# Emptying and clearing the PSUM banks of a graph kernel's counts two at a time

## The reference

```python
h = jnp.maximum(_layernorm(x), 0.0)
agg_src  = segment_sum(h[src], dst, 6250)          # round 0, features of the sources
agg_edge = segment_sum(edge_attr_128, dst, 6250)   # features of the edges
x = x + relu(concat([h, agg_src, agg_edge]) @ L0_W.T + L0_b)
h = jnp.maximum(_layernorm(x), 0.0)
for W_l, b, W_r in ((W1_l, b1, W1_r), (W2_l, b2, W2_r)):   # rounds 1 and 2
    agg = segment_sum(h[src], dst, 6250) / maximum(degree, 1)
    h = relu(agg @ W_l + b + h @ W_r)
x = x + h
```

## Time and profile before

| | us |
|---|---|
| median of 3 executions | 2033.34 |
| lowest, highest | 2031.09, 2033.35 |
| span of the profiled execution, first to last instruction | 1450.0 |
| the rest of the median, before and after the span | 583.3 |
| build, start of the first and of the last step (L997) | 120.8, 662.7 |
| TensorE matmul busy in the span | 1368.8 |
| ScalarE busy in the span | 490.1 |

### The profile page before, as it was taken

One profiled execution on the slowest core, in us unless ns is written; L12 is line 12 of the kernel. 1 busy time (PEld: TensorE's weight loads), 2 busy tenths in 40 slices (PEclk: granted clock), 3 DMA queues, 4 the chain that ended last, 5 costly groups with the idle time before them and its releaser, 6 DMA issues.

```text
span 1450.0 us, 34753 instructions
## 1 busy us (share of the span) xinstructions
PE 1368.8 (94%) x12165; PEld 1235.0 (85%) x12166; DVE 812.4 (56%) x1837; ACT 490.1 (34%) x1389; POOL 654.9 (45%) x772
## 2 busy tenths in 40 slices
PE   3777999999999999998999999999999999999996
PEld 3656999999999899997888888888888888888885
DVE  8686898888888888882454545432222222221221
ACT  2632123455688888882333232311111110000000
POOL 5400000011121121215777777167777745777775
PEclk9988999999999999999999999999999999999998
DMA  6108778888999988886565556566666665666663
GB/s 182 29 2 221 202 221 230 242 248 237 261 271 266 273 260 260 262 269 222 161 214 177 175 199 162 193 195 196 205 196 207 187 194 190 220 210 214 213 203 74
DMA packets 284762, 295.12 MB, mean 204 GB/s; under 512 B 19461, under 2 KB 250064, under 8 KB 284672
## 3 DMA queue, kind: packets, MB, share of 16 engines
q1 hardware_dynamic: 233861, 212.90, 46.9%
q0 software_dynamic: 26016, 69.24, 16.9%
q10 hardware_dynamic: 24795, 11.74, 2.8%
HBM read 245.70 MB, written 48.11 MB: 203 GB/s over the span
## 4 chain that ended last, share of the span: by engine, by line
PE 84%; POOL 2%; issue 2%; DMA 2%; ACT 2%; DVE 0%; ACTq 0%; POOLq 0%; DVEq 0%; SPq 0%
PE edge_banks L1065 41%; PE edge_banks L1023 20%; PE banks L997 10%; PE edge_banks L1096 4%; PE edge_banks L1019 4%; PE banks L1083 3%; POOL shared L833 2%; ACT shared L1252 1%; DMA shared<-in_edge_attr 1%; PE edge_banks L1072 1%; PE banks L1077 1%; ACT banks L1247 0%; DMA shared<-g_rows,list_src 0%; DMA shared<-counts 0%; ACT shared L1229 0%
## 5 line engine op out<-in xcount | busy, mean ns | idle before, releaser
L833 POOL DMA_INDIRECT shared<-g_rows,list_src x555 | 541.9, 976 | 230.8 <-issue 167.2
L1065 PE MATMUL edge_banks<-g_even,shared 128*128 128x257 f16 (+1 forms) x3822 | 444.7, 273 | 4.4 <-DMA shared<-counts 4.4
L1065 PEld LDWEIGHTS edge_banks<-g_even,shared 128*128 128x128 fp8e3 x3822 | 372.4, 97 | 62.6 <-issue 4.6
L1023 PE MATMUL edge_banks<-shared 128*128 128x128 f32 x2744 | 345.3, 277 | 4.4 <-issue 4.0
L1023 PEld LDWEIGHTS edge_banks<-shared 128*128 128x128 f32 x2744 | 325.8, 193 | 7.6 <-issue 7.0
L812 POOL DMA_DIRECT2D counts<-shared x156 | 76.4, 490 | 487.8 <-ACT shared L1252 472.8
L1639 DVE SCALAR_TENSOR_TENSOR shared<-edge_banks,shared,own 128x128 f32<-128x128 f32 x98 | 34.3, 350 | 367.6 <-PE edge_banks L1065 339.4
L1065 PE MATMUL edge_banks<-shared 128*128 128x256 f16 x1911 | 225.8, 272 | 0.2 <-DVE own L1621 0.2
L1551 DVE TENSOR_TENSOR shared<-iota,shared 128x3528 f16<-128x3528 f16 x98 | 195.5, 1995 | 51.2 <-PE banks L997 50.8
L1252 ACT ACTIVATE shared<-banks 128x392 uint16<-128x392 f32 x312 | 152.2, 488 | 184.6 <-PE banks L997 174.2
L1065 PEld LDWEIGHTS edge_banks<-shared 128*128 128x128 fp8e3 x1911 | 185.3, 97 | 30.7 <-DVE own L1621 0.5
(11 more groups left out here) (278 smaller groups left out, 997.6 us busy)
## 6 DMA issues: line engine op xcount, KB each, us to landing
shared<-in_edge_attr SPq DMA_DIRECT2D x195, 512.0 KB, 4.5
shared<-counts SPq DMA_DIRECT2D x117, 784.0 KB, 5.2
counts<-shared POOLq DMA_DIRECT2D x156, 196.0 KB, 3.8
shared<-g_rows,list_src POOLq DMA_INDIRECT x555
shared<-hot_rows SPq DMA_DIRECT2D x20, 304.0 KB, 2.9
g_rows<-g_even SPq DMA_DIRECT2D x1, 3136.0 KB, 15.5
g_rows<-shared ACTq DMA_DIRECT2D x49, 64.0 KB
g_rows<-g_even ACTq DMA_DIRECT2D x49, 64.0 KB
```

What stands on the lines that cost most here:

```text
L833: pool.indirect_dma_start(ring_g[use % RING][:, t, 0:2 * D], None, g_rows[r], bass.IndirectOffsetOnAxis(ap=list_src[:, at:at + 1], axis=0) ...
L1023: mm = pe.matmul(edge_wide[bank][:, :, at], ring[:, bank * GROUP_TILES + j, :], hot_dst[u][:, k, (j - 1) * SPREAD:j * SPREAD].unsqueeze(1) ...
L1065: mm = pe.matmul(acc[s][:, 0:wide], stream8[slot][:, order[h], :], G[r % 2][:, order[h], 0:wide], start=h == 0, stop=h == BLOCKS - 1, skip ...
```

## The change

A group of four windows (32 nodes, two banks) takes the place of a pair of windows (16 nodes, one bank) as the unit in which ScalarE empties and clears. The eight slots are now two halves of four slots (`HALVES`, `quad`). `step_done`, `evacuated`, the row sums and the table of ends count such groups of four: 156 where there were 312. Clearing adds 4 to `zeroed` at once. The stores of a block wait in two pairs in place of one by one. TensorE's steps, parts and waits keep their order and their values.

```diff
-        NDUO = DENSE * WINB // DUO
-        DPB = P // (WIN * DUO)
+        NQUAD = DENSE * WINB // QUAD
+        QPB = P // (WIN * QUAD)
...
-        duo = [banks[:, i, :].rearrange("p (w c) -> p w c", c=SLOT)[:, :, 0:CELLS] for i in range(BANKS)]
+        quad = [all_slots[:, i * QUAD * SLOT:(i + 1) * QUAD * SLOT].rearrange("p (w c) -> p w c", c=SLOT)[:, :, 0:CELLS] for i in range(HALVES)]
...
-                        pool.wait_ge(S["evacuated"], b * DPB + (DPB if isinstance(b, int) else DPB + k))
+                        pool.wait_ge(S["evacuated"], b * QPB + (QPB if isinstance(b, int) else QPB + k // 2))
...
-                        at, odd = (PER // 2 + j // 2, 1) if j % 2 == 0 else (j // 2, 0)
-                        mm = pe.matmul(flat[1][96:97, at:at + PER * (HOLDERS // 2 - 1) + 1:PER], c_end[:, j:j + 1],
-                                       identz[0:HOLDERS, 1 + odd:HOLDERS + odd:2], start=True, stop=True, skip_group_check=True)
+                        holder = (j + 1) % QUAD
+                        at = (PER * holder + j - (QUAD - 1)) // QUAD
+                        mm = pe.matmul(flat[1][96:97, at:at + PER * (HOLDERS // QUAD - 1) + 1:PER], c_end[:, j:j + 1],
+                                       identz[0:HOLDERS, 1 + holder:1 + HOLDERS:QUAD], start=True, stop=True, skip_group_check=True)
...
-            act.activation(ends_row, flat[1][96:97, 0:NDUO], ACT.Copy).then_inc(S["words_taken"], 1)
+            act.activation(ends_row, flat[1][96:97, 0:NQUAD], ACT.Copy).then_inc(S["words_taken"], 1)
...
-                        act.wait_ge(S["evacuated"], b * DPB + (j + 1))
-                        act.activation(duo[j % BANKS], zeros16[:, 0:1].unsqueeze(1).broadcast_to([P, DUO, CELLS]), ACT.Copy).then_inc(S["zeroed"], 2)
-                    for j in range(DPB):
+                        act.wait_ge(S["evacuated"], b * QPB + (j + 1))
+                        act.activation(quad[j % HALVES], zeros16[:, 0:1].unsqueeze(1).broadcast_to([P, QUAD, CELLS]), ACT.Copy).then_inc(S["zeroed"], QUAD)
+                    for j in range(QPB):
                         act.wait_ge(S["step_done"], regs[j])
-                        q = b * DPB + j
+                        q = b * QPB + j
...
-                        act.activation(stage_duo[s][:, :, j * WIN:(j + 1) * WIN].rearrange("p h (w d) -> p h w d", w=DUO),
-                                       duo[j % BANKS].rearrange("p w (d h) -> p h w d", h=BLOCKS), ACT.Copy,
+                        act.activation(stage_pairs[s][:, :, j * (QUAD * WIN // 2):(j + 1) * (QUAD * WIN // 2)].rearrange("p h (w d) -> p h w d", w=QUAD),
+                                       quad[j % HALVES].rearrange("p w (d h) -> p h w d", h=BLOCKS), ACT.Copy,
                                        accum_out=row_sum[:, qsl]).then_inc(S["evacuated"], 1)
```

More of the change, by code:

```diff
@@ L7 @@
 WIN = 8
-DUO = 2
+QUAD = 4
 BANKS = 4
+HALVES = 2
 SLOT = 256
@@ L88, in message_passing @@
     GW = 2 * D + 2
-    assert D == P and BLOCKS % 4 == 1 and LISTED % 2 == 0 and LBLK == 2 and CELLS <= SLOT and DPB % BANKS == 0 and NWIN == HOLDERS * PER and HOLDERS < P
+    assert D == P and BLOCKS % 4 == 1 and LISTED % 2 == 0 and LBLK == 2 and CELLS <= SLOT and QPB == 4 and HOLDERS % QUAD == 0 and NWIN == HOLDERS * PER and HOLDERS < P
     assert 0 < LEFT < P and SPAD <= 2048 and NSTEP < SPAD and FULLT - (TBLK - 1) * P < P - 8 and N < 1 << SRC_BITS
@@ L136, in message_passing @@
         bias_all = sb("bias_all", [P, 3, D])
-        row_sum = sb("row_sum", [P, NDUO])
+        row_sum = sb("row_sum", [P, NQUAD])
         norm_t = sb("norm_t", [P, 5 * BLOCKS])
@@ L175, in message_passing @@
         stage = [place(12596 + i * 1568, 1568).bitcast(U16) for i in range(2)]
-        stage_duo = [s.rearrange("p (h d) -> p h d", d=P // 2) for s in stage]
+        stage_pairs = [s.rearrange("p (h d) -> p h d", d=P // 2) for s in stage]
         a_tab = place(15732, SPAD // 2).bitcast(U16)
@@ L185, in message_passing @@
         bases = shared[64:65, 22068:22068 + NGROUP + 4].bitcast(I32)
-        ends_row = shared[96:97, 22068:22068 + NDUO].bitcast(I32)
-        assert SPAD <= 1792 and NTILE == 1568 and CELLS == 196 and NDUO == 312 and ROWS * ROWW <= 24496 - 22068
+        ends_row = shared[96:97, 22068:22068 + NQUAD].bitcast(I32)
+        assert SPAD <= 1792 and NTILE == 1568 and CELLS == 196 and NQUAD == 156 and ROWS * ROWW <= 24496 - 22068
         stream8 = [place(i * 1568, 1568).bitcast(F8).rearrange("p (h d) -> p h d", d=P) for i in range(4)]
@@ L203, in message_passing @@
         tiny = place(t0 + 9 * D + 224, 16).rearrange("p (s k) -> p s k", k=8)
-        low_i = place(t0 + 2 * D, NDUO).bitcast(I32)
-        high_i = place(t0 + 2 * D + NDUO, NDUO).bitcast(I32)
+        low_i = place(t0 + 2 * D, NQUAD).bitcast(I32)
+        high_i = place(t0 + 2 * D + NQUAD, NQUAD).bitcast(I32)
         r0 = t0 + 9 * D + 240
@@ L211, in message_passing @@
         list_hot_u8 = list_hot_u8.rearrange("p (t d) -> p t d", d=P)
-        assert r1 + RING * (MOST * GW // 2) <= SHARED and 2 * NDUO <= 6 * D and NLIST <= 10 * BLOCKS
+        assert r1 + RING * (MOST * GW // 2) <= SHARED and 2 * NQUAD <= 6 * D and NLIST <= 10 * BLOCKS
         tile_rows = place(0, TCOLS).bitcast(I32).rearrange("p (b e) -> p b e", e=P)
@@ L819, in rounds @@
                 pool.wait_ge(S["edges_ready"], 1)
-                pool.wait_ge(S["evacuated"], NDUO)
+                pool.wait_ge(S["evacuated"], NQUAD)
                 for q in range(RING):
@@ L1129, in rounds @@
                         if r == 0 and i == 1:
-                            pe.wait_ge(S["zeroed"], 2 * BANKS + 2 * NDUO)
+                            pe.wait_ge(S["zeroed"], 2 * BANKS + QUAD * NQUAD)
                         one(i)
@@ L1236, in build @@
             def build():
-                regs = registers(act, DPB, "end")
+                regs = registers(act, QPB, "end")
                 act.wait_ge(S["words_taken"], WORDS)
                 def evacuate(b, s, turn):
-                    act.load(regs, ends_row[:, b * DPB:(b + 1) * DPB] if isinstance(b, int) else ends_row[:, bass.ds(b * DPB, DPB)])
+                    act.load(regs, ends_row[:, b * QPB:(b + 1) * QPB] if isinstance(b, int) else ends_row[:, bass.ds(b * QPB, QPB)])
                     if not (isinstance(b, int) and b < 2):
@@ L1583, in check_sums @@
             def check_sums():
-                dve.wait_ge(S["evacuated"], NDUO)
+                dve.wait_ge(S["evacuated"], NQUAD)
                 link(dve.tensor_copy(low_i, row_sum[:, :]))
```

## The result

The changed kernel took 2056.3 us (median, 2052.8 to 2058.5) where the kernel before took 2033.3: a ratio of 1.0118, 95% interval 1.0104 to 1.0132. It is slower, as forecast, but by 23 us where 8 were forecast, and the time lies above the range.

A forecast was written before the change was run, and what follows sets the result against it. TensorE was taken to bound the build; stalls of 7.7 us, plus 1 us for restarts, less 0.6 us of present waits, gave +8 us, from 2033.3 to 2041 us, range 2034 to 2048.

The forecast's parts named there:

- What bounds the build: Build: TensorE bounds it throughout; true waits for ScalarE's clearing are about 0.6 us.
- something of the loop's start: Turns of TensorE's loop: 16 large gaps, some 10 us together, belong to the loop's start and not to ScalarE.
- if the loop's gaps change: Sign of being wrong: the gaps where turns of TensorE's loop begin change with the edit.
- ScalarE's durations: Build, ScalarE: evictions of four windows take 0.81 us and clearings 0.83, at 0.836 ns a column.
- The misaligned halves: Late build: TensorE waits for clearing inside halves at ten places, 7.7 us in sum.
- Parts costed at nothing: GpSimd's stores, final stores, copy of the ends and row-sum check: no cost, though two stores now leave together.
- What lies around the span: Outside the profiled span of 1450.0 us: 583.3 us to the median, untouched by the change.
- hidden: Rival: the ring still covers the eviction and nothing measurable happens; about 2035 us, chance 0.15.
- faster: Rival: gaps at the loop's start are ScalarE's or grow with its work, three quarters won; 2026 us, chance 0.12.
- Much slower: Rival: an instruction over two banks costs as much as two, some 50 parts wait, 20 to 25 us; chance 0.05.

The follow-up runs named there:

- a_again: The changed kernel once more, unchanged, against the kernel before: ratio 1.0161, 1472.3 us.
- b_again: The kernel before once more, unchanged, for a second profile: ratio 1.0000, 1450.4 us.
- evict_by_bank: The kernel before with each bank still evicted by itself, but two banks (four windows) cleared by one instruction: ratio 1.0051.
- stores_in_twos: The kernel before with GpSimd's pieces sent two and two, at the windows of the changed kernel: ratio 1.0069.
- stores_spread: The changed kernel with GpSimd's pieces waiting one by one, each for one more group of four: ratio 1.0098 against the kernel before.
- load_at_three: The kernel before with TensorE's register load two tiles, four matmuls, earlier in the edge matmuls (LOAD_AT = 3): ratio 1.0069.

## Why the prediction was wrong

*What bounds the build* was right. TensorE bounds it, ScalarE's clearing held up next to nothing, and the large gaps at the loop's start, put down to ScalarE by the profile, aren't waits for it. What they are is what the prediction left at "something of the loop's start": the register load there, as at `load_next`. In the profile before, TensorE goes on 0.42 us after the end of that load in all 18 of them over 0.15 us. That was the step at which to look further, since a load that leaves a gap now is a load whose time matters. The prediction's sign of being wrong, "if the loop's gaps change", looked at the wrong place: at the starts of turns they are 7.2 us in a_again and 7.4 in b_again, and those behind the loads in the edge matmuls grew.

*ScalarE's durations* were right: 0.82 and 0.83 us against 0.81 and 0.83. The slope of 0.836 ns a column held over four slots in two banks (0.85 for the eviction, 0.83 for the clearing). The Trainium skill ("ScalarE: Activation LUTs", section "What ACT_TABLE_LOAD costs") gives 0.833 ns a column, and the trace agrees. ScalarE is busy 65.6 us between 400 and 500 in a_again, forecast 65.

*The misaligned halves* were right in mechanism and in nine of ten places. That the sum was right too (7.5 us against 7.7) is in part luck, since misses of up to 0.9 us at single places cancel. In evict_by_bank they alone come with 0.5%.

*The step that failed* is the term "Parts costed at nothing": "The stores on GpSimd are as many, of the same size; two now leave together". I asked who waits for the stores, and found only ScalarE. I didn't ask what runs slower while they are in flight. What runs slower are the register loads of TensorE's sequencer, and the gaps behind them in the edge matmuls grew by 13.9 us of the build's 21.9. Sending in twos alone costs 9 us in the kernel before (stores_in_twos). In the changed kernel stores_spread wins 9 us back, with stores wider apart than before the change. A part of the gaps, 3.6 us, also comes with late clearing alone (evict_by_bank), and some 2 us only when both are there; why is open. The gaps also hide part of the waits for clearing, which are 12.4 us where the stores are spread. By what route a store slows a register load no run shows.

*What lies around the span* was wrong, 1.7 us in place of 583, but no term hung on it: the loss is 22 to 25 us where executions take 1450 us and 23 where they take 2033. Why some jobs hold TensorE back in the rounds stays open, and no run here was made on it.

*The rivals*: "hidden" and "faster" didn't come about. "Much slower" named the size (20 to 25 us) but not the mechanism, since two banks in one instruction don't cost as much as two instructions.

## What to carry to other kernels

Where a change moves transfers together in time, ask what slows down while they are in flight, and not only who waits for them; a sequencer's register load from SBUF is such a thing, and it shows in a trace as idle time without a releaser at a fixed place in the loop, or is put down to an engine that ended something by chance just before. When the unit in which a ring is freed doubles, lay the producer's bursts on the ring: the cost is in the few bursts that end one unit and need the next, not in the mean load of the engine that frees it. And compare the span with the time of the runs before anything is put between them: a difference of 583 us is another kind of execution, not a margin.

## What the runs showed of the hardware

- A load of twelve registers from SBUF by TensorE's sequencer took 0.84 us at least, 0.85 to 0.97 on the mean after 290 us with no store of GpSimd in flight, 1.2 in the kernel before and 1.3 to 1.4 with two stores at a time where store packets overlapped it, and up to 3.3 with four. Stores aren't the only thing that does it: two loads at 130.2 and 134.3 us in b_again took 2.5 and 2.9 us with none in flight, while the edge features came in.
- ScalarE's loads from SBUF took 0.55 us for eight registers (b_again) and 0.31 for four (a_again), and hardly varied (0.54 to 0.56 and 0.31 to 0.32). The Trainium skill ("DMA: Bandwidth & Descriptors", section "Latency and other measured facts") gives a floor of about 600 ns for a `tensor_load`. The loads of four and eight registers here were shorter, so the measurement decides.
- TensorE goes on with matmuls already queued while its sequencer waits for the load. Where such a load left a gap in the edge matmuls, ten or eleven had mostly started behind it, and no load of under 1.3 us left one of over 0.15 us (before, b_again); in load_at_three mostly seven had, and one of 0.96 us left a gap.
- In jobs of about 2033 us, idle times of up to 2.4 us with no releaser stood between TensorE's matmuls soon after the rounds began, and the granted clock went to and fro between its levels of 1.2 and 2.4 GHz, 0.79 on the mean from 700 us on, while the build before it ran at 0.99; the same kernels had 0.99 and no such gaps in jobs of 1450 us.
